# Squares for the guard from GpSimd to ScalarE, with GpSimd's queue and one VectorE step in another order, in an attention kernel between two spectral layers

## The chip, the cores and the metric

The kernel runs on one core of a Trainium2 chip. The metric is device time in microseconds (us) of one execution. Of the core's engines, TensorE (PE in the profile) multiplies into PSUM, ScalarE (ACT) takes exponentials, VectorE (DVE) does most elementwise work, GpSimd (POOL) does elementwise work between SBUF tensors, and SyncE (SP) issues nearly all DMAs.

## The reference

`x` is 8 batches of 512 tokens of 256 numbers. Everything is float32.

```python
x = x + 0.5 * ffn(layernorm(x))      # ffn: FFT over the 256, times a complex 256x256 matrix, real part of the inverse FFT, + bias
x = x + attention(layernorm(x))      # 16 heads of 8, on the left 128 columns; out @ Wo.T (128 -> 256) + bo
x = x + 0.5 * ffn(layernorm(x))
# attention: q, k, v = left @ Wq.T, left @ Wk.T, left @ Wv.T; softmax(q.k / 4) over all 512 keys; times v
```

## The kernel before

The complex matrix is turned once, at the start, into one real 256x256 matrix `half_ffn`, so that each ffn layer is a plain matrix product of 128x256 token tiles (jobs `F1_0` to `F1_3` for the first layer, `F2_0` to `F2_3` for the last, four tiles to a batch).

**Iterations and slots.** The main loop has 8 iterations, one for the attention of each batch. An iteration has 16 slots, one for each group of four heads and 128 keys. In slot `s` TensorE issues the scores of slot `s + 1` (`score_quad`, L768), then the jobs that the table `STEADY` (`BEGIN` in iteration 0, `END` in iteration 7) names for the slot, then the product of the exponentials of slot `s` with the values (`value_quad`, L781). ScalarE takes two exponentials of 128x1024 a slot (L637). There are three score buffers, so the scores of a slot wait for the first exponential of the slot before it.

**What a slot's jobs belong to.** Iteration `it` finishes batch `it - 1` (`WO_0` to `WO_3`, the output projection, in slots 2 and 3, `F2_0` to `F2_3` in slots 9 to 13), projects and checks batch `it + 1` (`QT_0` and `QT_1` in slots 7 and 8 make q, `N` in slot 10 and `NT` in slot 11 make a bound on its scores, and the two guards behind slot 12 branch on it), and begins batch `it + 2` (`F1_0` to `F1_3` in slots 0 to 6, its layernorm, and k in slots 14 and 15 by `KT_0` and `KT_1`). A job's result lies in one PSUM bank, `misc`; the jobs of a slot wait until VectorE has emptied it of those of the slot before (`evacuated`), and `NT` waits for the reduction `norms` (L981) that empties `N`.

**The guard.** `N` multiplies the bf16 squares of q and k (`sq_q`, `sq_k`) by a matrix of ones. Before, GpSimd makes the squares (`square`, L538, 128x512); each waits for VectorE's (`split`, L929) copies of q or k to SBUF.

**GpSimd's other work**, in an order written out by hand in its program, each step waiting for what it reads: `rstd_of(k, n)` (L527 and L529) is the power -0.5 of a variance, for the first (k = 0), the second (1) or the last (2) layernorm; `end_of(b)` (L542 and L532, 128x512 each) makes `x_out` from `x2` and a bias; `begin_x2(b)` (L542 and L532) makes `x2` from `x1` and a bias; `next_x(b)` (L542 and L532) adds a bias to an input.

**The left half.** VectorE normalizes the left 128 columns of batch `it + 2` in `left_half` (L903, four tiles of 128x128 into `lh`, two in slot 8 and two in slot 9, behind its wait for `rstd_of(1, it + 3)`), and turns them in `turn_left` (L912, into `left_blocks`). SyncE's queue, in program order, has `q_out` (q of batch `it + 1` to memory), `left_through` (L445, waits for `turn_left`), four DMAs of q back as rows (`q_rows`, L381, into `QS`), `leftT_in` (L452, which `KT_0` waits for), and four more `q_rows`. The scores of the next iteration's slot 0 wait for all of `QS` and `KS`.

**Divisions.** `normalize(it, 0)` (L1003, L1006: reciprocal, and product of `ot_t` and it into `on`) belongs to the first half of the attention output, which VectorE has turned in slot 7 and which is wanted after slot 15.

Of the kernel before, what the change touches and what calls it, by code (L numbers as in the profile page):

```python
# [25 lines left out]
ACT = mybir.ActivationFunctionType  # L26
AX = mybir.AxisListType

B, S, E = 8, 512, 256
# [3 lines left out]
T = S // P  # L33
# [18 lines left out]
PAIRS = 2 * QUADS  # L52
# [63 lines left out]
def evac_count(name, b):  # L116

    return INDEX[name, b] + 1
# [58 lines left out]
def build_macaron(nc, x, x_t, wq_t, wk_t, wv_t, wo_rows, bo, w_re, w_im, bias, cos_var, sin_tab, ident_in,  # L177
# [14 lines left out]
    with ctx:  # L192
# [44 lines left out]
        qp = sb("qp", [P, PARTS, S])  # L237
        kp = sb("kp", [P, PARTS, S])
        sq_q = sb("sq_q", [P, S], BF16)
# [95 lines left out]
        def wait(eng, s, value):  # L335

            if value > 0:
                eng.wait_ge(s, value)
# [174 lines left out]
        def _(pool):  # L513
# [22 lines left out]
            def square(parts, sq, step, b):  # L536
                pool.wait_ge(step, 2 * (b + 1))
                nc.gpsimd.tensor_tensor(sq[:, :], parts[:, 0, :], parts[:, 0, :], ALU.mult).then_inc(sq_done, 1)  # L538
# [4 lines left out]
                add_row(dst, src, row, done, slice(2, T))  # L543

            def end_of(b):
                wait(pool, out_stored, 32 * b)
                add_rows(x_out, x2, half_bias, x2b_done)

# [26 lines left out]
            pool.wait_ge(late_loaded, 32)  # L575
            begin_x2(0)
            next_x(2)
            square(kp, sq_k, kp_step, 1)
            square(qp, sq_q, qp_step, 1)
            rstd_of(1, 3)  # L580
            next_x(3)
            square(kp, sq_k, kp_step, 2)
            for it in range(1, B):
                rstd_of(2, it)
                if it + 2 < B:
                    rstd_of(1, it + 3)
                end_of(it - 1)
                if it + 1 < B:
                    square(qp, sq_q, qp_step, it + 1)
                begin_x2(it)  # L590
                if it + 3 < B:
                    next_x(it + 3)
                if it + 2 < B:
                    square(kp, sq_k, kp_step, it + 2)
            pool.wait_ge(out_stored, 32 * (B - 1))
            for i in range(2):
                pool.wait_ge(evacuated, evac_count(f"WO_{2 * i + 1}", B - 1))
# [4 lines left out]
        @block.scalar  # L602
        def _(act):
            act.dma_start(cos_var_sb[:, :, :], cos_var.rearrange("(c p) e -> p c e", p=P)).then_inc(re_loaded, 16)
            act.dma_start(sin_sb[:, :, :], sin_tab.rearrange("(c p) e -> p c e", p=P)).then_inc(im_loaded, 16)
            act.dma_start(bias_raw[:, :], bias.partition_broadcast(P)).then_inc(bias_loaded, 16)

            act.wait_ge(waking_set, 1)
            nc.scalar.activation(probs[0][:, 0, 0:32], waking[:, 0:32], ACT.Exp, scale=SCORE_SCALE)

            for piece, bank, copy in ((1, scores[0][:, 0], even[0]), (3, scores[1][:, 0], even[1])):
                act.wait_ge(ffn_mm, piece)
                nc.scalar.copy(copy[:, :, :], half_bank(bank)).then_inc(ffn_copied, 1)
            act.wait_ge(bias_loaded, 16)
            nc.scalar.mul(half_bias[:, :], bias_raw[:, :], 0.5).then_inc(bias_set, 1)
            for piece, bank, copy in ((5, scores[0][:, 0], even[2]), (6, scores[0][:, 1], odd)):
                act.wait_ge(ffn_mm, piece)
                nc.scalar.mul(copy[:, :, :], half_bank(bank), 0.5 / E).then_inc(ffn_copied, 1)


            act.wait_ge(misc_ready, ready_count("QT", 0))
            nc.scalar.copy(qp[:, 0, :].bitcast(F32R), bank_of("QT", 0)).then_inc(qp_step, 2)
            act.wait_ge(evacuated, evac_count("QT", 0))
            store_q(act)
            act.wait_ge(k_stored, 16)
            for lane in range(2, LANES):
                k_rows(act, 0, slice(0, 1), lane, first_rows_in)
            act.wait_ge(q_stored, 16)
            for lane in range(2, LANES):
                q_rows(act, 0, slice(0, 1), lane, first_rows_in)  # L630
            for lane in range(2, LANES):
                k_rows(act, 0, slice(1, SLOTS), lane, second_rows_in)

            for u in range(PAIRS * B):
                act.wait_ge(scores_ready, u // 2 + 1)
                wait(act, quad_done, (u - PRING) // 2 + 1)
                nc.scalar.activation(probs[u % PRING][:, :, :], scores[u % SRING][:, :, :], ACT.Exp,  # L637
                                     scale=SCORE_SCALE).then_inc(exp_done, 1)
            for i in range(2):
                act.wait_ge(lastT_ready, i + 1)  # L640
                nc.scalar.copy(xT[:, :, :, 2 * i:2 * i + 2, :].rearrange("p c g t s -> p (c g) (t s)"),
                               scores[0][:, i, :].rearrange("p (k s) -> p k s", s=2 * 32)).then_inc(lastT_copied, 1)
# [240 lines left out]
        def _(dve):  # L883
# [271 lines left out]
            for it in range(B):  # L1155
                for s in range(QUADS):
                    run_jobs(it, s)
                    if s == 7:
                        take_values(it, 0)
                    if s == 15:  # L1160
                        take_values(it, 1)
                    if s == 14:
                        normalize(it, 0)
                    if s == 0 and it >= 1:
                        normalize(it - 1, 1)
                    if it >= 1:
                        if s == 4:
                            for t in range(2):
                                norm_stats(2, x2, t, False)
                        if s == 5:  # L1170
                            for t in range(2, T):
                                norm_stats(2, x2, t, t == T - 1)
                            norm_moments(2, it)
                    else:
                        if s == 0:
                            norm0_stats(2, range(0, 2))
                        if s == 1:
                            norm0_stats(2, range(2, T))
                            norm_moments(0, 3)
                    if it + 2 < B:  # L1180
                        if s == 8:
                            left_half(it + 2, range(0, 2 if it else T))
                        if s == 9 and it:
                            left_half(it + 2, range(2, T))
                        if s == (9 if it else 8):
                            turn_left(it + 2)
                    if it + 3 < B:
                        if s == 11:
                            norm0_stats(it + 3, range(0, 2))
                        if s == 13:  # L1190
                            norm0_stats(it + 3, range(2, T))
                            norm_moments(0, it + 4)
                    if s == GUARD_SLOT and it + 1 < B:
                        guard(it + 1)
# [59 lines left out]
```

## Time and profile before

| | |
|---|---|
| runs | 338.58, 969.81 and 336.59 us, median 338.58 |
| the profiled execution | 335.66 us, its span 333.9 us |
| engine busy, share of span | PE 91%, ACT 75%, DVE 62%, POOL 34% |
| granted TensorE clock | full speed in all 40 slices |
| DMA | 50.40 MB, 151 GB/s on average; the packets of queue 1 take 52.1% of the 16 DMA engines' span |

The span is the time between the first and last instruction of the profiled execution; 1.8 us of its time lie outside. The main loop's slot-0 scores start at 35.0 us in iteration 0, and its last ones at 317 us, so that 85% of the span is main loop. An iteration of the steady kind (1 to 5) takes 36.4 to 37.5 us.

### The profile page before, as it was taken

The numbers are of one execution on the slowest core, as the hardware profiler recorded it, in microseconds if no ns is written. First come the engines' busy times: TensorE is split into PE (matmuls) and PEld (weight loads), VectorE is DVE, ScalarE is ACT, GpSimd is POOL, SyncE is SP. The second block draws the span as 40 slices with busy tenths as digits, with TensorE's granted clock in tenths as the row PEclk, the third lists the DMA queues.
The fourth block names the chain that finished last, engine by engine and source line by source line (L and its number), as shares of the span: only waits on it lengthen the run. The fifth ranks groups of instructions, "written<-read, shape, count | busy, mean of one in ns | idle before, by whom it ended". The sixth has DMA issues, their size and how long they took to land.

```text
span 333.9 us, 8968 instructions
## 1 busy us (share of the span) xinstructions
PE 302.7 (91%) x3477; PEld 115.7 (35%) x3481; DVE 208.2 (62%) x543; ACT 250.0 (75%) x266; POOL 112.6 (34%) x126
## 2 busy tenths in 40 slices
PE   8887799899988998989989998999988979898985
PEld 5543233234323332333323333343333223232333
DVE  2676656466886679676876778667955723461154
ACT  2100697998977889778978889798977997999921
POOL 5740461310635028140725036230901071007004
PEclk9999999999999999999999999999999999999999
DMA  7636959629535755748645955666354954112001
GB/s 207 221 128 198 183 130 246 194 85 167 204 135 145 186 141 213 213 141 156 232 128 157 167 146 209 203 161 127 128 159 161 139 160 146 65 41 87 33 34 63
DMA packets 30389, 50.40 MB, mean 151 GB/s; under 512 B 3841, under 2 KB 16513, under 8 KB 29441
## 3 DMA queue, kind: packets, MB, share of 16 engines
q1 hardware_dynamic: 28864, 48.13, 52.1%
q10 hardware_dynamic: 1472, 1.58, 2.1%
q8 instruction: 32, 0.52, 0.7%
q14 instruction: 21, 0.16, 0.2%
HBM read 31.87 MB, written 17.83 MB: 149 GB/s over the span
## 4 chain that ended last, share of the span: by engine, by line
PE 51%; DVE 16%; DMA 15%; SPq 7%; issue 6%; ACT 3%; POOL 1%; DVEq 0%; ACTq 0%; POOLq 0%
PE misc L687 20%; PE ot L781 18%; PE scores L768 9%; SPq L381 6%; DVE lh L903 6%; DMA QS<-q_scr 4%; DMA xT<-x_scr 3%; DMA leftT<-left_scr 3%; DMA x_scr<-x_blocks 3%; ACT probs L637 2%; DMA x_in<-x 2%; DVE left_blocks L912 2%; PE scores L687 2%; DVE stats L885 1%; POOL rstd L529 1%
## 5 line engine op out<-in xcount | busy, mean ns | idle before, releaser
L637 ACT ACTIVATE probs<-scores 128x1024 f32<-128x1024 f32 x256 | 244.8, 1027 | 50.4 <-PE scores L768 50.2
L781 PE MATMUL ot<-probs,VS 128*32 128x512 f32 x1024 | 135.6, 595 | 5.0 <-ACT probs L637 3.7
L768 PE MATMUL scores<-QS,KS 32*128 32x512 f32 x512 | 65.0, 495 | 4.6 <-DMA QS<-q_scr 3.7
L527 POOL TENSOR_SCALAR veps<-mv 128x4 f32<-128x4 f32 (+1 forms) x25 | 5.7, 227 | 171.9 <-DVE mv L892 171.9
L768 PEld LDWEIGHTS scores<-QS,KS 32*128 32x128 f32 x512 | 24.7, 181 | 111.8 <-ACT probs L637 96.1
L781 PEld LDWEIGHTS ot<-probs,VS 128*32 128x32 f32 x1024 | 31.1, 109 | 28.4 <-ACT probs L637 9.4
L687 PE MATMUL misc<-half_ffn,xT 128*32 128x256 f32 x448 | 31.4, 385 | 8.0 <-DVE norms L981 6.0
L963 DVE SCALAR_TENSOR_TENSOR x_out<-misc,rstd,x_out 128x256 f32<-128x256 f32 x28 | 13.5, 482 | 33.6 <-PE misc L687 27.4
L687 PE MATMUL misc<-half_ffn,xT_in 128*32 128x256 f32 x400 | 27.9, 385 | 1.4 <-DVE half_ffn L1130 1.3
L903 DVE TENSOR_SCALAR lh<-x,mv,rstd 128x128 f32<-128x128 f32 x32 | 26.2, 868 | 1.8 <-POOL rstd L529 1.8
L529 POOL TENSOR_TENSOR rstd<-veps,power 128x4 f32<-128x4 f32 (+1 forms) x25 | 25.2, 1008 | 2.1
L885 DVE BATCH_NORM_STATS2 stats<-x 128x6 f32<-128x256 f32 x64 | 23.4, 412 | 0.1
L939 DVE SCALAR_TENSOR_TENSOR x<-misc,rstd,x_in 128x256 f32<-128x256 f32 x24 | 11.6, 484 | 15.2 <-PE misc L687 15.2
L958 DVE TENSOR_TENSOR x<-misc,x 128x256 f32<-128x256 f32 x30 | 11.3, 420 | 15.3 <-PE misc L687 15.3
L687 PEld LDWEIGHTS misc<-half_ffn,xT 128*32 128x32 f32 x448 | 11.4, 108 | 19.1 <-DVE norms L981 7.6
L532 POOL TENSOR_TENSOR x_out<-x,half_bias 128x512 f32<-128x512 f32 x9 | 11.5, 1283 | 17.9 <-DVE x L958 17.9
L998 DVE STREAM_TRANSPOSE ot_t<-ot 128x512 f32<-128x512 f32 x16 | 11.4, 714 | 9.0 <-PE ot L781 9.0
L687 PE MATMUL misc<-wo_sb,otn 128*32 128x256 f32 x240 | 16.1, 385 | 0.6 <-DVE otn L1012 0.6
L918 DVE STREAM_TRANSPOSE x_blocks<-x 128x512 f32<-128x512 f32 x14 | 16.2, 1157 | 0.5
L661 PE MATMUL scores<-waking 128*128 128x512 bf16 x49 | 13.0, 412 | 2.5 <-issue 1.3
L538 POOL TENSOR_TENSOR sq_k<-kp 128x512 bf16<-128x512 f32 x8 | 8.3, 1041 | 18.2 <-DVE kp L929 18.2
L687 PEld LDWEIGHTS misc<-half_ffn,xT_in 128*32 128x32 f32 x400 | 10.3, 109 | 11.0 <-issue 5.4
(111 smaller groups left out, 273.3 us busy)
## 6 DMA issues: line engine op xcount, KB each, us to landing
KS<-k_scr SPq DMA_DIRECT2D x56, 128.0 KB, 4.9
QS<-q_scr SPq DMA_DIRECT2D x56, 128.0 KB, 3.3
x_in<-x SPq DMA_DIRECT2D x8, 512.0 KB, 6.0
xT_in<-x_t SPq DMA_DIRECT2D x8, 512.0 KB, 6.8
k_scr<-kp SPq DMA_DIRECT2D x8, 512.0 KB, 2.6
q_scr<-qp SPq DMA_DIRECT2D x7, 512.0 KB, 3.4
x_scr<-x_blocks SPq DMA_DIRECT2D x7, 512.0 KB, 3.6
xT<-x_scr SPq DMA_DIRECT2D x7, 512.0 KB, 4.6
```

What stands on the lines that cost most here:

```text
L381: eng.dma_start(QS[par][first:ROWS * (lane + 1):PARTS, slots, :], q_scr[:, :, heads, :].rearrange("i d h s -> (i d) h s")).then_inc(loaded ...
L529: nc.gpsimd.tensor_tensor(to[:, tiles], veps[k][:, tiles], power[:, tiles], ALU.pow).then_inc(rstd_done[k], 1)
L637: nc.scalar.activation(probs[u % PRING][:, :, :], scores[u % SRING][:, :, :], ACT.Exp, scale=SCORE_SCALE).then_inc(exp_done, 1)
L661: mm(bank, waking[:, 0:P], waking[:, :], start=True, stop=True)
L687: last = mm(dst[COL * j:COL * (j + 1), :], weights(j), rhs, start=c == 0, stop=c == len(terms) - 1)
L768: last = mm(scores[(u + j // 2) % SRING][:, j % 2, :], KS[b % 2][rows, slot, kt * P:(kt + 1) * P].bitcast(F32R), QS[b % 2][rows, slot, :]. ...
L781: last = mm(ot[COL * j:COL * (j + 1), :], VS[b % 2][:, kt, h, :], probs[(u + j // 2) % PRING][:, j % 2, :], start=s % 8 == 0, stop=s % 8 == 7)
L885: ins = nc.vector.bn_stats(stats[k][:, t, :], src[:, t, :])
L903: last = nc.vector.tensor_scalar(lh[:, t, :], x1[b % 3][:, t, 0:HD], mv[1][:, t, 0:1], rstd[1][0][:, t:t + 1], ALU.subtract, ALU.mult)
L918: last = nc.vector.transpose(x2_blocks[:, :, 2 * i:2 * i + 2, :], x2[:, 2 * i:2 * i + 2, :].rearrange("p t (f k) -> p k t f", k=E // 32))
L939: return nc.vector.scalar_tensor_tensor(x1[b % 3][:, i, :], tile, rstd[0][b % 2][:, i:i + 1], biased[:, i, :], ALU.mult, ALU.add)
L963: nc.vector.scalar_tensor_tensor(x_out[:, i, :], tile, rstd[2][0][:, i:i + 1], x_out[:, i, :], ALU.mult, ALU.add).then_inc(evacuated, 1)
```

## The change

Three things are changed. First, the squares of batches 1 to 7 leave GpSimd: ScalarE makes each by one `Square` activation, in iteration `it` for batch `it + 1`, that of k ahead of the exponentials of slot 2 (slot 4 in iteration 0) and that of q ahead of those of slot 10 (slot 6 in iteration 0). Second, in GpSimd's loop `end_of` comes ahead of `rstd_of(2, it)` and waits for `WO_3`, and `begin_x2` comes directly behind that, ahead of `rstd_of(1, it + 3)`. Third, VectorE does `normalize(it, 0)` in slot 12 and no longer in slot 14.

```diff
             def end_of(b):
+                pool.wait_ge(evacuated, evac_count(f"WO_{T - 1}", b))
                 wait(pool, out_stored, 32 * b)
                 add_rows(x_out, x2, half_bias, x2b_done)
...
             next_x(2)
-            square(kp, sq_k, kp_step, 1)
-            square(qp, sq_q, qp_step, 1)
             rstd_of(1, 3)
             next_x(3)
-            square(kp, sq_k, kp_step, 2)
             for it in range(1, B):
+
+                end_of(it - 1)
                 rstd_of(2, it)
+                begin_x2(it)
                 if it + 2 < B:
                     rstd_of(1, it + 3)
-                end_of(it - 1)
-                if it + 1 < B:
-                    square(qp, sq_q, qp_step, it + 1)
-                begin_x2(it)
                 if it + 3 < B:
                     next_x(it + 3)
-                if it + 2 < B:
-                    square(kp, sq_k, kp_step, it + 2)
...
+            def square(parts, sq, step, b):
+                act.wait_ge(step, 2 * (b + 1))
+                nc.scalar.activation(sq[:, :], parts[:, 0, :], ACT.Square).then_inc(sq_done, 1)
+
             for u in range(PAIRS * B):
+                it, s = divmod(u, PAIRS)
+                if it + 1 < B:
+
+                    if s == (2 * 2 if it else 2 * 4):
+                        square(kp, sq_k, kp_step, it + 1)
+                    if s == (2 * 10 if it else 2 * 6):
+                        square(qp, sq_q, qp_step, it + 1)
                 act.wait_ge(scores_ready, u // 2 + 1)
...
-                    if s == 14:
+                    if s == 12:
                         normalize(it, 0)
```

GpSimd's queue in iteration 1, before, from the last square of iteration 0 to the start of `next_x`. `veps` and `rstd` rows are `rstd_of`, `x_out<-x` is `end_of`, `x<-x_1,bo_sb` is `begin_x2`.

```order
L538 TENSOR_TENSOR sq_k<-kp 128x512
L527 TENSOR_SCALAR veps<-mv 128x4
L529 TENSOR_TENSOR rstd_0<-veps,power 128x4
L527 TENSOR_SCALAR veps<-mv 128x4
L529 TENSOR_TENSOR rstd_0<-veps,power 128x4
L542 TENSOR_TENSOR x_out<-x,half_bias 128x512
L532 TENSOR_TENSOR x_out<-x,half_bias 128x512
L538 TENSOR_TENSOR sq_q<-qp 128x512
L542 TENSOR_TENSOR x<-x_1,bo_sb 128x512
L532 TENSOR_TENSOR x<-x_1,bo_sb 128x512
L527 TENSOR_SCALAR veps<-mv 128x4
```

The same place in the changed kernel:

```order
L542 TENSOR_TENSOR x_out<-x,half_bias 128x512
L532 TENSOR_TENSOR x_out<-x,half_bias 128x512
L527 TENSOR_SCALAR veps<-mv 128x4
L529 TENSOR_TENSOR rstd_0<-veps,power 128x4
L542 TENSOR_TENSOR x<-x_1,bo_sb 128x512
L532 TENSOR_TENSOR x<-x_1,bo_sb 128x512
L527 TENSOR_SCALAR veps<-mv 128x4
L529 TENSOR_TENSOR rstd_0<-veps,power 128x4
L527 TENSOR_SCALAR veps<-mv 128x4
```

The power that the left half waits for (the second `rstd` row of each) now stands behind all four large additions of the iteration, where it stood ahead of them, and nothing stands between it and the `veps` of `next_x`.

ScalarE's queue from its last DMA of the start to iteration 2; a row with x16 is eight slots of exponentials. The lines marked - are before, those marked + the changed kernel.

```order
 L374 DMA KS<-k_scr 16x3x512 x4
-L637 ACTIVATE probs<-scores 128x1024 x256
-L641 COPY xT<-scores 128x8x64 x2
+L643 ACTIVATE probs<-scores 128x1024 x8
+L631 ACTIVATE sq_k<-kp 128x512
+L643 ACTIVATE probs<-scores 128x1024 x4
+L631 ACTIVATE sq_q<-qp 128x512
+L643 ACTIVATE probs<-scores 128x1024 x24
+L631 ACTIVATE sq_k<-kp 128x512
+L643 ACTIVATE probs<-scores 128x1024 x16
+L631 ACTIVATE sq_q<-qp 128x512
```

Fourteen squares stand among the exponentials, where there was nothing, and no other row is new.

VectorE's queue at the end of an iteration (slots 13 to 15), before:

```order
L963 SCALAR_TENSOR_TENSOR x_out<-misc,rstd_0,x_out 128x256
L885 BN_STATS stats<-x_in 128x6 x2
L892 BN_AGGR mv<-stats 128x2 x4
L929 CAST kp<-misc 128x256
L931 TENSOR_TENSOR kp<-misc,kp 128x256
L1003 RECIPROCAL recip<-ot_t 128x32
L1006 TENSOR_TENSOR on<-ot_t,recip 128x16x16
L929 CAST kp<-misc 128x256
```

The same place in the changed kernel:

```order
L969 SCALAR_TENSOR_TENSOR x_out<-misc,rstd_0,x_out 128x256
L891 BN_STATS stats<-x_in 128x6 x2
L898 BN_AGGR mv<-stats 128x2 x4
L935 CAST kp<-misc 128x256
L937 TENSOR_TENSOR kp<-misc,kp 128x256
L935 CAST kp<-misc 128x256
```

The two rows of `normalize` have left the place between the two halves of k; they stand one slot after `NT`, ahead of the branch of the guard.

## Rows read from the trace of the kernel before

**Rows 1.** The profile's page: busy time, share of the span, instructions.
```profile
PE 302.7 (91%) x3477; PEld 115.7 (35%) x3481; DVE 208.2 (62%) x543; ACT 250.0 (75%) x266; POOL 112.6 (34%) x126
```

**Rows 2.** Waits of the whole execution: us in total, times, longest.
```profile
PEld scores L768 <- DMA QS<-q_scr: 8.1, 6, 2.5
...
PE misc L687 <- DVE norms L981: 6.0, 5, 1.3
```

**Rows 3.** Timeline of TensorE, iteration 2: start us, us, what, [idle before <-releaser].
```profile
131.68 0.51 PE L768 MATMUL scores<-QS,KS 32*128 32x512 f32 x4
...
135.11 0.51 PE L768 MATMUL scores<-QS,KS 32*128 32x512 f32 x4
...
139.71 0.51 PE L768 MATMUL scores<-QS,KS 32*128 32x512 f32 x4
...
143.26 0.50 PE L768 MATMUL scores<-QS,KS 32*128 32x512 f32 x4 [1.62 <-DMA QS<-q_scr]
```

**Rows 4.** Timeline of VectorE, iteration 2, slots 8 to 10.
```profile
126.68 0.42 DVE L929 CAST qp<-misc 128x256 fp32r<-128x256 f32 x1 [0.29 <-PE misc L687]
...
127.48 2.03 DVE L903 TENSOR_SCALAR lh<-x,mv,rstd 128x128 f32<-128x128 f32 x2
129.43 0.47 DVE L963 SCALAR_TENSOR_TENSOR x_out<-misc,rstd,x_out 128x256 f32<-128x256 f32 x1
129.83 2.17 DVE L903 TENSOR_SCALAR lh<-x,mv,rstd 128x128 f32<-128x128 f32 x2
132.03 1.10 DVE L912 STREAM_TRANSPOSE left_blocks<-lh 128x512 f32<-128x512 f32 x1
133.04 0.39 DVE L981 TENSOR_REDUCE norms<-misc 128x1 f32<-128x256 f32 x1
```

**Rows 5.** Timeline of GpSimd, iteration 2, slots 6 to 10.
```profile
122.94 1.04 POOL L529 TENSOR_TENSOR rstd<-veps,power 128x4 f32<-128x4 f32 x1
...
124.90 1.02 POOL L529 TENSOR_TENSOR rstd<-veps,power 128x4 f32<-128x4 f32 x1
125.90 1.29 POOL L542 TENSOR_TENSOR x_out<-x,half_bias 128x512 f32<-128x512 f32 x1
...
130.60 1.30 POOL L532 TENSOR_TENSOR x<-x,bo_sb 128x512 f32<-128x512 f32 x1
```

**Rows 6.** Line L903 in iteration 0 (GpSimd idle), then 88 to 250 us: duration ns min/median/max.
```profile
L903 DVE TENSOR_SCALAR lh<-x,mv,rstd x4: 341/343/347, 57.1 to 57.8; 128x128 f32<-128x128 f32 x4
...
L903 DVE TENSOR_SCALAR lh<-x,mv,rstd x20: 922/1056/1323, 90.5 to 241.3; 128x128 f32<-128x128 f32 x20
```

**Rows 7.** Timeline of the DMA issues of SyncE, iteration 2.
```profile
133.15 0.33 SPq L445 DMA_DIRECT2D left_scr<-left_blocks  x1
133.53 3.05 SPq L381 DMA_DIRECT2D QS<-q_scr  x4
136.69 0.52 SPq L452 DMA_DIRECT2D leftT<-left_scr  x1
```

**Rows 8.** ScalarE's groups of instructions: count, busy us, mean ns of one.
```profile
L609 ACT ACT_TABLE_LOAD x1 | 1.3, 1283 | 2.3 <-issue 2.3
...
L622 ACT CAST qp<-scores 128x512 fp32r<-128x512 f32 x1 | 0.6, 586 | 12.5 <-PE scores L687 12.5
```

**Rows 9.** Timeline of ScalarE, iteration 2.
```profile
124.23 5.71 ACT L637 ACTIVATE probs<-scores 128x1024 f32<-128x1024 f32 x6 [0.35 <-PE scores L768]
130.29 3.88 ACT L637 ACTIVATE probs<-scores 128x1024 f32<-128x1024 f32 x4 [0.35 <-PE scores L768]
135.67 1.94 ACT L637 ACTIVATE probs<-scores 128x1024 f32<-128x1024 f32 x2 [1.50 <-PE scores L768]
```

**Rows 10.** Timeline of iteration 4, slot 9 and the turn behind it.
```profile
202.55 1.07 PE L687 MATMUL misc<-half_ffn,xT 128*32 128x256 f32 x16 [0.34 <-DMA xT<-x_scr]
...
206.27 1.10 DVE L912 STREAM_TRANSPOSE left_blocks<-lh 128x512 f32<-128x512 f32 x1
```

## The prediction, as it was put on record

> **What bounds the kernel now.** First the busy shares of the page: TensorE has 91% and ScalarE 75% [rows 1], so time is won only where TensorE waits, and work given to ScalarE must fit into what it has left. Then the waits of the whole execution [rows 2], for what TensorE waits for and how often. Two waits recur once an iteration: for the rows of q (`QS`), 8.1 us in six waits of the weight loads that go ahead of the scores, and for `norms`, 6.0 us in five. Then the timelines of one iteration, of which I take iteration 2.
>
> In TensorE's timeline [rows 3] slots 12 and 13 are two undisturbed slots with 16 job multiplications: 139.71 - 135.11 = 4.60, 2.30 us each. Slot 11 is a light one, but takes 135.11 - 131.68 = 3.43 us. Slot 14, with eight job multiplications, takes 143.26 - 139.71 = 3.55 us, and its row says that the scores had waited 1.62 us for `QS`. Without a wait a light slot goes by ScalarE: six exponentials in a row take 5.71 us [rows 9], so two take 1.90.
>
> VectorE's timeline [rows 4] shows what both waits hang on. In slots 8 and 9 it makes the four tiles of the left half, 2.03 and 2.17 us for two each, then turns them until 133.13, and only then takes `norms`, until 133.43, which frees `misc` for the jobs of slot 11. SyncE stores `left_blocks` at 133.15, and the first `QS` rows, which stand behind that store in its queue, go out at 133.53, `leftT` at 136.69, the last `QS` rows behind it [rows 7]. The last of them lands just ahead of 143.26. So from the end of the turn to the next iteration it is 143.26 - 133.13 = 10.1 us, in which nothing is waited for but transfers, and an iteration of the steady kind is as long as this chain makes it.
>
> And the left half is slow for one reason. A tile took 0.343 us in iteration 0, where GpSimd did nothing, and 1.056 us in the median of the twenty of iterations 1 to 5 [rows 6]. GpSimd is without a pause in its additions and a square from 125.90 to 130.60 + 1.30 = 131.90 [rows 5], and the tiles run from 127.48 to 132.00. So a tile waits for GpSimd's instructions, some three times its own time. Other VectorE work that lies beside GpSimd's, as the evacuation of 0.47 us at 129.43, isn't longer.
>
> **GpSimd's new order.** In iteration 2 `rstd_of(2)` ends at 122.94 + 1.04 = 123.98 [rows 5]. Now `end_of` is done before it, in slots 3 and 4, and `begin_x2` follows: two additions of 1.25 us from start to start, until 126.5. Then `rstd_of(1)`, 0.3 us for `veps` and 1.02 for the power: 127.8. That is 1.9 us later than its 125.92. VectorE is free for the left half at 127.5, so the first pair begins 0.3 us later, at 127.85. From there GpSimd has nothing to do until `next_x` in slot 13, since the squares are gone. The pair takes 0.6 us (0.343, and the next some 0.25 behind it, as the four of iteration 0 start from 57.1 to 57.8), until 128.45. The second pair stands behind the evacuation of `F2_0`, which the first pair no longer holds up; TensorE's product for it ends about 129.0, so it is emptied by 129.5. Second pair until 130.05, turn of 1.10 us [rows 4] until 131.2. Before it was 133.13: **1.9 us earlier**.
>
> `norms` is then done at about 131.6, while the jobs of slot 11 want it at 131.68 + 0.45 [rows 3]: that wait is gone, and slot 11 falls from 3.43 to about 2.1 us, a gain of 1.3. The q rows come 1.9 us earlier, so the next iteration can begin at 141.35. TensorE by itself would be there at 139.71 - 1.3 + 1.9 = 140.3. What is late next is therefore the same chain, and the iteration is shorter by the whole 1.9 us, 1.3 in slot 11 and 0.6 in slot 14. The first q rows can't be read before q itself is in memory; they were issued 6 us behind the last copy of q, and I take that a store of a few us is done 4 us behind it as well.
>
> This holds for iterations 1, 2, 3 and 5, 4 x 1.9 = 7.6 us. In iteration 4 `F2_0` waited for `xT` and began at 202.55 [rows 10]. It is emptied by 204.15 whatever GpSimd does, so the turn ends at 205.85 and not at 206.27 + 1.10 = 207.37: 1.5 us. Iteration 0 has fast tiles already [rows 6], and iterations 6 and 7 have no left half: nothing. **Sum 9.1 us.** The Trainium skill (GPSIMD Engine Reference, Key points) has the contention with VectorE only for instructions in a two-port mode or with two SBUF inputs. By that rule the turns of `x2` in slots 2 and 3, which now meet `end_of`, are slowed only if they run in such a mode, which no row here shows; see the third rival.
>
> **The squares on ScalarE.** The trace has no square on this engine. The nearest row is its copy of 128x512 in 0.586 us [rows 8]; exponentials of 1.03 us in the mean stand 0.95 apart in a row (5.71 / 6), so I take 0.51 us for one among others. The lower bound is the same copy without its start, some 0.43, the upper one 0.59: 14 squares are 6 to 8.3 us of ScalarE. What lies over them: a full slot takes 2.30 us and its two exponentials 1.90 to 1.94, so that ScalarE idles some 0.35 us ahead of a pair [rows 9], and the next scores need the first exponential alone. The square of k stands ahead of slot 2, at the beginning of five to seven such slots; it pushes the exponentials by 0.15 to 0.2 us, which nobody waits for and the next gap takes back. **Nothing.** The square of q stands in the run of six exponentials from 124.23, ahead of its fifth, at 128.04. It waits for the copy of q, which ends at 126.68 + 0.42 = 127.10 [rows 4], so there is 0.9 us to spare. It pushes the run by 0.51, of which 0.35 is the gap before the next run [rows 9], and the remaining 0.2 lies in slots 10 to 13, where the chain of the q rows sets the end. **Nothing**; without that cover it would be 0.2 an iteration. `N` needs the square in slot 10, two slots of exponentials before which it is done. In iteration 6 slots 0 and 1 are ScalarE's, and I put 0.2 us there. Off GpSimd the squares give nothing of their own beyond what the left half was given above. The Trainium skill (ScalarE: Activation LUTs, Rules for kernel authors) speaks against this: `mul` belongs on VectorE, not ScalarE. By its formula in "What ACT_TABLE_LOAD costs" a square of 512 is about 0.61 us, an estimate, near the row's 0.586; 14 of them with no cover would take all but some 0.6 us of the gain.
>
> **The division in slot 12.** Two VectorE rows leave slot 14 for slot 12, where VectorE has nothing but an evacuation of 0.47 us in 2.30. In slot 14 they lay between the two halves of k, but the second half is multiplied only behind the scores at 143.26 [rows 3], when they were done. Nothing. The new wait on `WO_3` holds only GpSimd's own queue, which had to wait for the same data anyway.
>
> So 9.1 - 0.2 = 8.9 us, against the profiled execution's 335.66: 326.8. The other two undisturbed runs are 336.59 and 338.58; I take 336.6 as what the kernel before does, which gives **327.6 us**, 2.7% less. A measurement of this kernel can tell about 2% from no change.
>
> **The rivals.**
> First, the transfers don't follow. Between the turn and the last q row lie a store, a load and eight row loads with the DMA engines half busy; moved up by 1.9 us they meet more of the loads of `x` and the store of q. If each iteration loses 0.9 of its 1.9 us, 5 x 0.9 = 4.5, it is 332. For it: this chain measured from 9 to 10 us in different iterations. Against: its steps are mostly the fixed time of an issue and a landing. If nothing of slot 14 moves at all and the chain ends where it did, it eats the gain of slot 11 too, and the time is 336.6.
> Second, ScalarE becomes the bound, on the other side. Place: the run from slot 8 to slot 12. Price: 14 x 0.59 = 8.3 us with none covered; it decides from the point where the square of q is reached before its copy is there, that is if VectorE is over 0.9 us later than now, or the chain of the q rows is not what ends the iteration. Without any gain elsewhere that is 344.9. For it: 75% busy, and six exponentials in a row with no gap. Against: gaps of 0.35 and 1.50 us on both sides [rows 9]. A harder form is that a square throws out the table of the exponential. A table load took 1.283 us [rows 8]; two to a square and the square itself are 14 x 3.15 = 44 us, less 9 of gain: 372. Against: the changed program has no more such loads in ScalarE's queue than the one before. The same page of the Trainium skill (Table sets: the hidden batching unit) has a load at a switch to another set only, puts relu, copy, identity and abs into every set, and doesn't say of square; by its figure of about 2.66 us for each switch it would be more than this.
> Third, `end_of` beside the turns of `x2`. No such turn lay beside GpSimd's work in this trace. If VectorE's turn waits as a tile does, `x2` is out up to 1.1 us later, and so is `xT` at `F2_0`: 1.1 in iterations 4 and 6, which wait for it already, and little in the others: 2.5 us, 330.1.
> Fourth, the q rows come even sooner, because the later part of the chain took 10.1 us in iteration 2 and may take 9 everywhere: some 3 us more, 324.5.
>
> **How the numbers follow.** Forecast 0.66 (its own range 325 to 330), transfers that follow in part 0.12 (332), not at all 0.07 (336.6), the turns 0.05 (330.1), ScalarE as the bound 0.04 (344.9), table loads 0.02 (372), better 0.04 (324.5). The range 324 to 333 takes in the forecast, the fourth, the third and the partial one, 0.87. Faster by over 2% is below 329.9: nearly all of the forecast, the fourth, and parts of the first and third, 0.74; slower 0.06; the rest 0.20.
>
> **What would show it.** Tiles of the left half at 0.34 us, no wait for `norms`, slot 11 near 2.1 us, the first q rows 1.9 us earlier against slot 8, squares of 0.5 to 0.6 us on ScalarE with no table load, `begin_x2` between the two powers. What would make it wrong: a wait for `QS` that grows by as much as the one for `norms` shrinks, slots 8 to 11 longer than 1.9 us with ScalarE full, or longer turns of `x2`.

## The result and the profile after

The changed kernel takes 327.62 us in the median of four runs (326.72 to 328.11). The kernel before took 336.59, 338.58, 353.86 and 969.81 us, and ratios, here and below, leave out runs over 1.5% above the fastest of their kernel, here the last two, while times are medians of all runs. The ratio is 0.9702 with a 95% interval of 0.9641 to 0.9762: 3.0% faster. A second set of six runs of the same kernel, further down, gives 0.9743 (0.9684 to 0.9803). The forecast was 327.6 us and 2.7%. The profiled execution took 327.63 us, 8.0 less than the 335.66 of the one before.

The page of the changed kernel, part 1, answers to [rows 1]:

```profile
PE 302.9 (93%) x3477; PEld 116.5 (36%) x3481; DVE 191.9 (59%) x543; ACT 255.4 (78%) x280; POOL 97.7 (30%) x112
```

GpSimd has 14 instructions less and is busy 14.9 us less, ScalarE 14 more and 5.4 us longer. VectorE has the instructions that it had, and yet is busy 16.3 us less: most of it are the twenty tiles of the left half, which [rows 6] has at 1.06 us.

The waits, to [rows 2] (us in total, times, longest):

```profile
PEld scores L774 <- DMA QS<-q_scr: 5.9, 6, 1.7
...
PE misc L693 <- DMA leftT<-left_scr: 2.7, 4, 1.1
...
PE scores L774 <- DMA QS<-q_scr: 1.7, 2, 0.9
...
PE misc L693 <- DMA xT<-x_scr: 1.7, 2, 1.0
```

The row of `norms` is gone, that of `QS` is smaller and still the largest of this kind, and `leftT` has 2.7 us. That last wait isn't new. The kernel before had it too, with one wait less, in a row that [rows 2] leave out:

```profile
PE misc L687 <- DMA leftT<-left_scr: 2.5, 3, 1.5
```

VectorE's tiles, to [rows 6], for 88 to 250 us:

```profile
L909 DVE TENSOR_SCALAR lh<-x,mv,rstd x20: 339/343/350, 91.2 to 234.5; 128x128 f32<-128x128 f32 x20
```

All twenty take the 0.34 us that those of iteration 0 took. Iteration 2 on VectorE, to [rows 4]; its slot-0 scores are at 104.61 (105.73 before):

```profile
126.70 0.61 DVE L909 TENSOR_SCALAR lh<-x,mv,rstd 128x128 f32<-128x128 f32 x2 [0.27 <-POOL rstd L529]
127.88 0.48 DVE L969 SCALAR_TENSOR_TENSOR x_out<-misc,rstd,x_out 128x256 f32<-128x256 f32 x1 [0.58 <-PE misc L693]
128.28 0.59 DVE L909 TENSOR_SCALAR lh<-x,mv,rstd 128x128 f32<-128x128 f32 x2
128.91 1.17 DVE L918 STREAM_TRANSPOSE left_blocks<-lh 128x512 f32<-128x512 f32 x1
129.99 0.41 DVE L987 TENSOR_REDUCE norms<-misc 128x1 f32<-128x256 f32 x1
```

The turn ends 130.08 - 104.61 = 25.47 us into the iteration; before it was 133.13 - 105.73 = 27.40. So it is 1.93 us earlier, and 1.9 was forecast. TensorE, to [rows 3]:

```profile
130.55 0.51 PE L774 MATMUL scores<-QS,KS 32*128 32x512 f32 x4
132.61 0.51 PE L774 MATMUL scores<-QS,KS 32*128 32x512 f32 x4
134.90 0.50 PE L774 MATMUL scores<-QS,KS 32*128 32x512 f32 x4
137.19 0.51 PE L774 MATMUL scores<-QS,KS 32*128 32x512 f32 x4
138.23 0.64 PE L693 MATMUL misc<-leftT,wk_sb 128*32 128x256 f32 x8 [0.53 <-DMA leftT<-left_scr]
139.66 0.51 PE L774 MATMUL scores<-QS,KS 32*128 32x512 f32 x4
```

Slot 11 takes 132.61 - 130.55 = 2.06 us, where it took 3.43. Slot 14 takes 139.66 - 137.19 = 2.47, where it took 3.55, and what its row names now is `leftT`, not `QS`. The last q row isn't far off: issued at 135.8, it lands 9.3 us behind the turn, at 139.4. So without the wait for `leftT` the slot-0 scores could have begun some 0.25 us earlier, not more. GpSimd and ScalarE in the same stretch:

```profile
125.30 0.24 POOL L527 TENSOR_SCALAR veps<-mv 128x4 f32<-128x4 f32 x1
125.63 1.04 POOL L529 TENSOR_TENSOR rstd<-veps,power 128x4 f32<-128x4 f32 x1
```

```profile
123.09 3.80 ACT L643 ACTIVATE probs<-scores 128x1024 f32<-128x1024 f32 x4 [0.35 <-PE scores L774]
126.78 0.63 ACT L631 ACTIVATE sq_q<-qp 128x512 bf16<-128x512 f32 x1
127.30 7.82 ACT L643 ACTIVATE probs<-scores 128x1024 f32<-128x1024 f32 x8
135.47 1.94 ACT L643 ACTIVATE probs<-scores 128x1024 f32<-128x1024 f32 x2 [0.35 <-PE scores L774]
```

GpSimd's last work ahead of the tiles ends at 126.67. The square of q stands among the exponentials without a gap on either side, 0.63 us long by its record, and moves them by 127.30 - 126.78 = 0.52 us, where 0.51 was taken. There is no table load beside it. It turns the runs of six and four exponentials into one of twelve with the square in it, from 123.09 to 135.12, and only behind that is ScalarE waiting again. The turns of `x2`, half of which now lie beside `end_of`, took 1.15 to 1.18 us, and 1.14 to 1.17 before.

The slot-0 scores of iterations 1 to 6 stand at 69.10, 104.61, 139.66, 174.87, 209.91 and 246.24; before, at 68.79, 105.73, 143.26, 179.99, 216.41 and 253.83. Iterations 1 to 5 took 177.1 us together and took 185.0 before: 7.9 us of the 8.0.

### The profile page after: what moved, and what is told of

Same layout as the page of the kernel before. It is cut to its first block, busy times and chain, and to the rows that moved or that the text cites. A ratio compares the mean times of both kernels' runs of the same rounds, so it can differ in the third digit from the quotient of the medians.

```text
span 325.8 us, 8974 instructions
## 1 busy us (share of the span) xinstructions
PE 302.9 (93%) x3477; PEld 116.5 (36%) x3481; DVE 191.9 (59%) x543; ACT 255.4 (78%) x280; POOL 97.7 (30%) x112
## 4 chain that ended last, share of the span: by engine, by line
PE 61%; DMA 12%; DVE 10%; issue 6%; SPq 5%; ACT 4%; POOL 1%; DVEq 0%; ACTq 0%; POOLq 0%
PE misc L693 22%; PE ot L787 21%; PE scores L774 11%; DMA leftT<-left_scr 6%; SPq L381 4%; ACT probs L643 4%; DMA xT<-x_scr 3%; DVE lh L909 2%; PE scores L660 2%; DVE left_blocks L918 2%; PE scores L693 2%; DMA x_scr<-x_blocks 1%; PE scores L667 1%; DMA QS<-q_scr 1%; DVE stats L891 1%
## 5 line engine op out<-in xcount | busy, mean ns | idle before, releaser
L542 POOL TENSOR_TENSOR x_out<-x,half_bias 128x512 f32<-128x512 f32 x7 | 9.0, 1291 | 98.5 <-DVE x L964 98.5
L969 DVE SCALAR_TENSOR_TENSOR x_out<-misc,rstd,x_out 128x256 f32<-128x256 f32 x28 | 13.5, 484 | 34.6 <-PE misc L693 25.6
L945 DVE SCALAR_TENSOR_TENSOR x<-misc,rstd,x_in 128x256 f32<-128x256 f32 x24 | 11.6, 484 | 15.1 <-PE misc L693 15.1
L532 POOL TENSOR_TENSOR x_out<-x,half_bias 128x512 f32<-128x512 f32 x9 | 11.5, 1282 | 20.6 <-DVE x L964 20.6
L1004 DVE STREAM_TRANSPOSE ot_t<-ot 128x512 f32<-128x512 f32 x16 | 11.4, 715 | 10.2 <-PE ot L787 10.2
L924 DVE STREAM_TRANSPOSE x_blocks<-x 128x512 f32<-128x512 f32 x14 | 16.3, 1162 | 0.5
L693 PEld LDWEIGHTS misc<-half_ffn,xT 128*32 128x32 f32 x448 | 11.4, 108 | 12.4 <-issue 8.4
L935 DVE CAST kp<-misc 128x256 fp32r<-128x256 f32 x14 | 5.9, 424 | 16.6 <-PE misc L693 16.6
```

The lines of the kernel that those rows point to most:

```text
L532: nc.gpsimd.tensor_tensor(dst[:, tiles, :], src[:, tiles, :], row[:, :].unsqueeze(1).to_broadcast([P, tiles.stop - tiles.start, E]), ALU.a ...
L693: last = mm(dst[COL * j:COL * (j + 1), :], weights(j), rhs, start=c == 0, stop=c == len(terms) - 1)
L924: last = nc.vector.transpose(x2_blocks[:, :, 2 * i:2 * i + 2, :], x2[:, 2 * i:2 * i + 2, :].rearrange("p t (f k) -> p k t f", k=E // 32))
L945: return nc.vector.scalar_tensor_tensor(x1[b % 3][:, i, :], tile, rstd[0][b % 2][:, i:i + 1], biased[:, i, :], ALU.mult, ALU.add)
L969: nc.vector.scalar_tensor_tensor(x_out[:, i, :], tile, rstd[2][0][:, i:i + 1], x_out[:, i, :], ALU.mult, ALU.add).then_inc(evacuated, 1)
```

## The experiments

Theory A is the prediction's: the tiles of the left half are slow beside GpSimd's work, and the chain of transfers behind them sets the length of an iteration. Its rivals are that the squares themselves were what counted (B), that GpSimd's earlier results were (C), and that ScalarE's time counts wherever a square stands (D). The kernels of one group ran on the same chip beside the kernel before: the first four below, then the changed kernel once more with the one without squares and the first two on transfers, then the last two on transfers with the division in its old place. Every ratio is to that, with its 95% interval.

### GpSimd's order without the squares' move

```diff
 # the changed kernel, but in the program of GpSimd
                 begin_x2(it)
                 if it + 2 < B:
                     rstd_of(1, it + 3)
+                if it + 1 < B:
+                    square(qp, sq_q, qp_step, it + 1)
                 if it + 3 < B:
                     next_x(it + 3)
+                if it + 2 < B:
+                    square(kp, sq_k, kp_step, it + 2)
 # ... and no squares in that of ScalarE
```

> The changed kernel with the squares back on GpSimd: that of q behind rstd_of(1), that of k at the end of the iteration; GpSimd's new order and the division in slot 12 stay. Theory A (the tiles of the left half are slow beside GpSimd's work, and the chain behind them sets the length of an iteration): one square of 1.04 us lies beside the first pair of tiles alone, whose time is hidden until F2_0 is evacuated, so nearly all of the gain stays, 327.6 to 328.8 us. Theory B (the gain is that GpSimd and N get rid of the squares): 334 to 337 us.

329.04 us, ratio 0.9771 (0.9722 to 0.9820). Nearly all of the gain is there. Of an iteration's four tiles the first alone is slow, as the maximum shows, and the time of the first pair is hidden until `F2_0` comes:

```profile
L905 DVE TENSOR_SCALAR lh<-x,mv,rstd x20: 330/334/1060, 90.6 to 234.0; 128x128 f32<-128x128 f32 x20
```

Theory B falls as the explanation of the whole gain. What the move of the squares gives beside the order is less than these runs can tell.

### The squares' move without GpSimd's order

```diff
 # the changed kernel, but in the program of GpSimd
             for it in range(1, B):
-                end_of(it - 1)
                 rstd_of(2, it)
-                begin_x2(it)
                 if it + 2 < B:
                     rstd_of(1, it + 3)
+                end_of(it - 1)
+                begin_x2(it)
 # ... and normalize(it, 0) back in slot 14
```

> The squares on ScalarE, but GpSimd's order and the place of the division as before the change. Theory A: end_of and begin_x2 still lie beside the left half, 5.1 us of them and no longer 6.0, so the turn ends some 0.9 us earlier than before in each of five iterations: 336.6 - 4.5, 331 to 333 us. Theory B: all of the gain, about 327.6 us.

333.56 us, ratio 0.9879 (0.9832 to 0.9926), between both kernels, as theory A has it. GpSimd is done one square earlier beside the left half, so that most tiles are slow still, but the last of an iteration are not:

```profile
L908 DVE TENSOR_SCALAR lh<-x,mv,rstd x20: 334/808/1323, 92.3 to 240.6; 128x128 f32<-128x128 f32 x20
```

### Nothing but work for GpSimd beside the left half

```diff
                 if it + 2 < B:
                     rstd_of(1, it + 3)
+                    for n in range(4):
+                        pool.wait_ge(idle_set, 4 * (it - 1) + n + 1)
+                        nc.gpsimd.tensor_tensor(idle[:, :], idle_in[:, :], idle_in[:, :], ALU.add).then_inc(idle_set, 1)
```

> The changed kernel with four additions of 128x512 on GpSimd behind rstd_of(1), into a tile that nobody reads, in iterations 1 to 5: nothing waits for them. Theory A: 4 x 1.3 us of GpSimd's work lie beside the left half again, tiles go from 0.34 to some 1.05 us, norms and the q rows are late again: 335 to 337.5 us. Theory C (the gain is that x_out and x2 are ready earlier, or that the powers are): unchanged, 327 to 328 us, since next_x isn't delayed.

337.94 us, ratio 1.0016 (0.9987 to 1.0045). Four additions whose result nobody reads, in a queue that has nothing else to do then, take back the whole gain. The additions stand first, then VectorE's turn in iteration 2, which began at 107.97, and the tiles of iterations 1 to 5, then the waits:

```profile
130.01 4.40 POOL L594 TENSOR_TENSOR idle<-idle_in 128x512 f32<-128x512 f32 x4
```

```profile
134.53 1.09 DVE L925 STREAM_TRANSPOSE left_blocks<-lh 128x512 f32<-128x512 f32 x1
```

```profile
L916 DVE TENSOR_SCALAR lh<-x,mv,rstd x20: 802/1128/1198, 92.3 to 244.9; 128x128 f32<-128x128 f32 x20
```

```profile
PEld scores L781 <- DMA QS<-q_scr: 8.9, 6, 2.4
...
PE misc L700 <- DVE norms L994: 5.8, 5, 1.2
```

The turn ends 135.62 - 107.97 = 27.65 us into the iteration, the 27.40 of the kernel before and a little more, and both waits of [rows 2] are back, though `x_out`, `x2` and all powers are as early as in the changed kernel: in iteration 2 `end_of` starts 11.17 us in (11.16 there), `begin_x2` 18.23 (18.21), and the power for the left half 21.03 (21.02). Theory C falls. This run shows the cause and not only that it fits: the tiles, and with them the time, follow GpSimd's work alone.

### Every square twice

```diff
                 act.wait_ge(step, 2 * (b + 1))
+                nc.scalar.activation(sq_spare[:, :], parts[:, 0, :], ACT.Square)
                 nc.scalar.activation(sq[:, :], parts[:, 0, :], ACT.Square).then_inc(sq_done, 1)
```

> The changed kernel with every square on ScalarE made twice, the first one into a tile that nobody reads. Theory A (a square is covered by ScalarE's gap of 0.35 us a full slot and by the chain of the q rows): 0 to 1.5 us more, 327.5 to 329 us. Theory D (ScalarE is the bound wherever a square stands): 14 x 0.52 = 7.3 us more, 335 us.

329.54 us, ratio 0.9779 (0.9734 to 0.9825). Its profiled execution has the second square in iteration 2, and the slots that it touches:

```profile
127.30 0.63 ACT L632 ACTIVATE sq_spare<-qp 128x512 bf16<-128x512 f32 x1
127.82 0.63 ACT L633 ACTIVATE sq_q<-qp 128x512 bf16<-128x512 f32 x1
128.34 7.59 ACT L645 ACTIVATE probs<-scores 128x1024 f32<-128x1024 f32 x8
136.29 1.94 ACT L645 ACTIVATE probs<-scores 128x1024 f32<-128x1024 f32 x2 [0.36 <-PE scores L776]
```

```profile
126.83 0.50 PE L776 MATMUL scores<-QS,KS 32*128 32x512 f32 x4
...
129.42 0.51 PE L776 MATMUL scores<-QS,KS 32*128 32x512 f32 x4 [0.23 <-ACT probs L645]
...
138.03 0.51 PE L776 MATMUL scores<-QS,KS 32*128 32x512 f32 x4
...
139.90 0.51 PE L776 MATMUL scores<-QS,KS 32*128 32x512 f32 x4
```

Slot 9 takes 129.42 - 126.83 = 2.59 us, not 2.29: 0.3 us in which TensorE waits for an exponential, and so in each of iterations 1 to 5. With 0.35 us in slot 3 of iteration 0 and 0.5 in slot 1 of iteration 6 the fourteen further squares cost TensorE 2.4 us of their 7.3. Slot 14 of iteration 2 then takes 139.90 - 138.03 = 1.87, not 2.47. That it takes the 0.3 us back is likely but not shown by this slot: a second trace of the changed kernel, without a doubled square, has 1.92 there. Over iterations 1 to 5 slot 14 takes 12.3 us here, 13.5 and 12.7 in the two traces of the changed kernel. Theory D (335 us) falls, and the second square is covered for the most part.

### No squares at all

```diff
-                    pe.wait_ge(sq_done, 2 * (b + 1))
+                    pe.wait_ge(sq_done, 2)
 # ... and no squares of batches 1 to 7 in any program
```

> The changed kernel without the squares of batches 1 to 7 on any engine: N multiplies those of batch 0 again, so this part of the computation is left out. Theory A (squares are covered): at most 0.5 us less than the changed kernel, from iteration 6. Theory D (ScalarE's time counts): 14 x 0.52 = 7.3 us less, 320 us.

329.31 us, ratio 0.9763 (0.9700 to 0.9825). The changed kernel itself, once more beside it:

> The changed kernel as it is, beside the next ones on the same chip: 327 to 329 us.

328.83 us, ratio 0.9743 (0.9684 to 0.9803). Without the squares nothing is won that these runs can tell. The one place where a trace has it is slot 1 of iteration 6: 1.87 us without, 2.03 with the square. Slots 9 to 13 of iteration 2, around the square of q, take 10.9 us with it and without it.

### The division back in slot 14

```diff
-                    if s == 12:
+                    if s == 14:
                         normalize(it, 0)
```

> The changed kernel with the division of the first half back in slot 14. Theory A has it at nothing: 327 to 329 us, as the changed kernel. The rival is that it held up the second half of k beside next_x's additions, 0.1 to 1 us an iteration in four to five iterations: 330 to 332 us.

328.34 us, ratio 0.9776 (0.9726 to 0.9826): no difference of its own in the median. But the trace has what the prediction put at nothing. VectorE and GpSimd, and the scores that TensorE issues in slots 0 and 1 of iteration 5, whose slot-0 scores were at 210.79:

```profile
211.23 1.40 DVE L1012 TENSOR_TENSOR on<-ot_t,recip 128x256 f32<-128x256 f32 x1
212.31 1.46 POOL L532 TENSOR_TENSOR x_in<-x_in,half_bias 128x512 f32<-128x512 f32 x1
212.55 0.41 DVE L935 CAST kp<-misc 128x256 fp32r<-128x256 f32 x1
212.65 0.51 PE L774 MATMUL scores<-QS,KS 32*128 32x512 f32 x4
213.00 0.42 DVE L937 TENSOR_TENSOR kp<-misc,kp 128x256 fp32r<-128x256 f32 x1
...
213.48 0.64 PE L693 MATMUL misc<-wv_sb,leftT 128*32 128x128 f32 x16 [0.32 <-DVE kp L937]
...
215.34 0.50 PE L774 MATMUL scores<-QS,KS 32*128 32x512 f32 x4
```

The product `on` takes 1.40 us beside `next_x` (0.42 to 0.43 in all sixteen of the changed kernel), the second half of k waits for it, and slot 0 takes 215.34 - 212.65 = 2.69 us and not 2.30, 0.39 us more. At the start of iterations 3 and 4 it is 0.07 and 0.26 us, of iteration 2 none. It goes with where the product ends: 0.78 us behind the slot-0 scores of iteration 2, then 1.52, 1.71 and 1.84.

### The chain of transfers behind the turn

In the changed kernel slot 14 waits for `leftT` in iterations 2 to 5, the four waits of its row above. Two kernels take up how the transfers stand in their queues.

```diff
                 if it + 1 < B:
-                    q_in(it + 1, range(0, 2))
+                    q_in(it + 1, range(0, 1))
                 if it + 2 < B:
                     leftT_in(it + 2)
                 if it + 1 < B:
-                    q_in(it + 1, range(2, LANES))
+                    q_in(it + 1, range(1, LANES))
```

> The changed kernel with leftT's DMA two q rows earlier in SyncE's queue. In the trace of the changed kernel slot 14 of iterations 2 and 4 ends by leftT, not by the last q row. Theory E (leftT is what ends it there): 0.3 to 0.5 us less in each of two iterations, about 0.8 us in all, no more, since the last q rows come when they came or 0.3 us later. Theory F (the q rows are the bound everywhere): no change or up to 1.5 us more.

326.42 us, ratio 0.9667 (0.9611 to 0.9724), 2.4 us less than the changed kernel of the same group, with intervals that overlap. A second time it was 325.78, 0.9683 (0.9638 to 0.9729):

> The changed kernel with leftT two q rows earlier, once more, as the base of the next one: 325 to 327 us.

Theory F falls. The gain is more than the 0.8 us of theory E, which counted iterations 2 and 4 alone. In the traces slot 14 takes 11.4 and 11.6 us over iterations 1 to 5, where the two of the changed kernel have 13.5 and 12.7: 1.1 to 2.0 us less. The DMA issues, size and median time to landing, of the changed kernel and of this one:

```profile
leftT<-left_scr SPq DMA_DIRECT2D x6, 256.0 KB, 5.1
```

```profile
leftT<-left_scr SPq DMA_DIRECT2D x6, 256.0 KB, 3.3
```

`leftT` isn't only issued earlier, it also lands faster, and no wait for it is left. What ends slot 14 now is the last q row, in each of the five iterations. The second kernel gives four of the eight q rows to GpSimd's queue as well:

```diff
                     rstd_of(1, it + 3)
+                if it + 1 < B:
+                    pool.wait_ge(quad_done, QUADS * it)
+                    pool.wait_ge(q_stored, 16 * (it + 2))
+                    for lane in range(2, LANES):
+                        q_rows(pool, (it + 1) % 2, slice(0, SLOTS), lane, pool_rows_in)
```

> The changed kernel with the last four q rows of an iteration issued by GpSimd, which has nothing to do between the power for the left half and next_x, and with leftT two rows earlier in SyncE's queue. Theory G (the chain is SyncE's issue time, eight rows at 0.6 us): all rows are in before slot 15, slot 14 goes by ScalarE with 1.9 us, and 2.91 + 2.46 + 2.60 + 2.44 + 3.04 - 5 x 1.9 = 4.0 us are won against the changed kernel, 323 to 324 us. Theory H (transfers are limited by the DMA engines or GpSimd's own issue takes as long): 326 to 329 us, or more where GpSimd's issue falls beside the tiles of the left half.

329.72 us, ratio 0.9785 (0.9726 to 0.9845). All is issued by 134.4 in iteration 2, which began at 105.03, and yet slot 14 takes 2.78 us there and waits for `leftT` in every iteration:

```profile
130.42 2.03 POOL L382 DMA_DIRECT2D QS<-q_scr  x4 [3.33 <-DMA q_scr<-qp]
```

```profile
PE misc L703 <- DMA leftT<-left_scr: 3.8, 5, 1.0
```

```profile
QS<-q_scr POOLq DMA_DIRECT2D x28, 128.0 KB, 3.8
QS<-q_scr SPq DMA_DIRECT2D x28, 128.0 KB, 4.5
...
leftT<-left_scr SPq DMA_DIRECT2D x6, 256.0 KB, 5.7
```

A q row of SyncE lands in 4.5 us and not 3.2, `leftT` in 5.7 and not 3.3. The q rows as a whole are in somewhat sooner: the last one lands 8.9 us behind the turn in iteration 2, where it was 9.3 in the changed kernel and 9.1 with `leftT` earlier. But `leftT` lands 8.3 us behind it, where it was 8.0 and 5.4. Theory G, that the issue time is the limit, falls: what is saved in issuing goes into longer transfers (H).

Last, the base with `leftT` earlier, and all four tiles in slot 8:

```diff
-                            left_half(it + 2, range(0, 2 if it else T))
-                        if s == 9 and it:
-                            left_half(it + 2, range(2, T))
+                            left_half(it + 2)
```

> The former with all four tiles of the left half in slot 8, where GpSimd is now idle. Four tiles take 1.2 us, from 0.1 us after the last half of q to just before F2_0 is to be evacuated, so the turn ends about 0.55 us earlier than with two of them behind F2_0. Theory A (the chain from the turn to the last q row sets the iteration): up to 0.5 us less in each of five iterations as far as slot 14 is over ScalarE's 1.9 us, 1.3 us in all, 324.5 to 326 us. Theory I (q's own store, which is done at about the same time, starts the chain): no change.

325.10 us, ratio 0.9646 (0.9596 to 0.9696), the fastest of all. It is 0.7 us below its base, within the intervals, so the times don't decide between theories A and I. The traces say more. The turn ends 24.8 us into each of iterations 1 to 5, 0.7 earlier than in the base (25.5). SyncE's queue in iteration 3, here (slot-0 scores at 140.79, end of the turn at 165.59) and in the base (138.99 and 164.48):

```profile
166.65 1.14 SPq L381 DMA_DIRECT2D QS<-q_scr  x2
```

```profile
164.88 1.14 SPq L381 DMA_DIRECT2D QS<-q_scr  x2
```

The first q row goes out 25.86 us into the iteration and 25.89 in the base: it has gained nothing, since q's own store is done only 1.0 us behind the turn. In iterations 2 and 4 more than half of the 0.7 us is lost in this way, in 1 and 5 none. Iterations 1 to 5 take 173.8 us together and 174.6 in the base: 0.8 less, where theory A had up to 1.3. So each theory holds for a part, and q's store is the next thing in the way.

This is 3.5% less than the kernel before. Against the changed kernel (0.9702, 0.9641 to 0.9762) it is 0.6%, which these runs don't make certain.

## What the prediction had right and what it had wrong, step by step

The mechanism was right. What failed is a size: the term of 9.1 us, and in it the step "the iteration is shorter by the whole 1.9 us, 1.3 in slot 11 and 0.6 in slot 14".

**The bound and the cause** are shown. Tiles at 0.34 us, no wait for `norms`, the turn 1.93 us earlier (1.9), slot 11 at 2.06 us (2.1): each as put down, and the run with idle additions shows that GpSimd's work beside the tiles is the cause.

**What an iteration gains** was mis-sized. Iteration 2 lost 37.53 - 35.05 = 2.48 us, the other four 1.43, 1.52, 1.38 and 1.09, together 7.9 where the term was 9.1. Slot 11 gave its part, 6.4 us in the five. Slot 14 did not: it lost 1.08 us in iteration 2, but 0.06, 0.18, 0.03 and 0.44 in 1, 3, 4 and 5, where 0.6 was put down. The step took the chain from the turn to the next slot-0 scores to stay as long as it was. The sums over iterations 1 to 5, in us, of the kernel before and of two traces of the changed kernel (the second is that of the run beside the one without squares):

| | before | changed | changed, again |
|---|---|---|---|
| slot-0 scores to the end of the turn | 136.9 | 128.1 | 127.3 |
| end of the turn to the next slot-0 scores | 48.1 | 49.0 | 48.4 |
| together | 185.0 | 177.1 | 175.7 |

The turns came 8.8 us earlier, and the chain behind them took 0.9 us more. In the second trace it is 9.6 and 0.3, and the gain is 9.3. So the term was 1.2 us too large for one execution and 0.2 too small for another of the same kernel: the chain in iteration 2 took 10.1 us before, then 9.6 and 9.1. The first rival had this scatter as its reason. Why it varies stays open. Its steps aren't of a fixed time, as the prediction had it: in iterations 1 to 5 of the traces with all q rows on SyncE `leftT` alone took 2.8 to 5.9 us to land.

**What is late next** was given as the q rows alone. In iterations 2 to 5 it was `leftT`, by 0.2 to 0.4 us. It took 5.1 us to land there in the median, and 3.16 in iteration 2 of the kernel before, the one that I had looked at; in iterations 3 to 5 of that kernel it took 4.5 to 5.4 and was waited for already.

**Iteration 4 and `xT`.** The 0.4 us that `xT` cost in iteration 4 of [rows 10] wasn't there; in iteration 5 it was 0.7 us in its place, and in the second trace none. The term of 1.5 us belonged to one execution, not to one iteration.

**The squares** cost nothing where nothing was forecast, and 2.03 - 1.87 = 0.16 us in slot 1 of iteration 6 where 0.2 was. The reason given for the square of q was not the one: its 0.2 us were to be hidden by the chain of the q rows in slot 14, but they never reach TensorE, since slots 9 to 13 take as long without the squares. ScalarE catches up in its own gaps. Only a second square gets through, 0.3 us in slot 9.

**The division** was put at nothing, because the second half of k is multiplied only behind the scores at 143.26, "when they were done". They weren't. The kernel before has, beside `next_x`,

```profile
142.03 1.47 DVE L1006 TENSOR_TENSOR on<-ot_t,recip 128x256 f32<-128x256 f32 x1
```

which ends at 143.50 and takes over three times its own 0.42 us. At the start of iterations 2, 4 and 5 it ends 0.8 to 1.3 us behind the slot-0 scores. It cost nothing there, since VectorE takes the second half of k only at 144.41, and has waited 0.91 us for it by then. In the kernel with the division back in slot 14 and the rest of the change, the product ends up to 1.84 us behind the slot-0 scores, and costs up to 0.4 us in an iteration.

**The sum.** 8.9 us was forecast and 8.0 came in the profiled execution, 335.66 to 327.63. That the time was met to 0.1 us is luck in part: it rests on the start taken as 336.6 (and 336.6 - 8.9 is 327.7). From the profiled execution alone the forecast would have been 326.8; and against the 337.6 that 336.59 and 338.58 have in the mean, 10.1 us were won.

**The rivals.** Neither slower one came: no table load, and ScalarE, with twelve exponentials and a square in a row, still waited behind them. The turns of `x2` didn't get longer beside GpSimd's additions. "Transfers that follow in part" is true by a size: 0.9 us of 9 in one trace, 0.3 in the other.

## What to carry to other kernels

When an instruction takes three times its own time in one place and not in another, look at what a neighbour engine does in those microseconds: work that nobody waits for can cost as much as work on the critical path. Moving it costs nothing if a stretch is free, and the check is an experiment that adds idle work there. One trace is one execution: a term that is read from a single iteration of it should be read from all of them, and from a second trace where there is one. And an edit costed at nothing because a wait covers it has to be costed again against the profile in which the other edits have removed that wait.

## What the runs showed of the hardware

- Beside GpSimd's additions between SBUF tiles, a VectorE `TENSOR_SCALAR` of 128x128 float32 in SBUF took 1.06 us in the median for 0.34 (kernel before), and a `TENSOR_TENSOR` of 128x256 in SBUF 1.16 to 1.46 for 0.42 (division back in slot 14). Not longer were evacuations from PSUM with one SBUF operand (0.48 us), `BATCH_NORM_STATS2` (0.41) and 32x32 transposes of 128x512 between SBUF tiles (1.17 for 1.16), of which the kernel before had shown nothing. The Trainium skill (GPSIMD Engine Reference, Key points) has contention for two-port modes and two SBUF inputs. The `TENSOR_TENSOR` with two SBUF inputs agrees with it; for the `TENSOR_SCALAR`, with one, it would take a two-port mode, which no row here shows.
- A `Square` of 128x512 to bf16 on ScalarE had a record of 0.63 to 0.64 us and cost 0.52 between exponentials, without a table load.
- How long a DMA takes to land depends on what is issued around it: `leftT` (256 KB) took 3.3 us in the median with two q rows ahead of it in its queue, 5.1 with four, and 5.7 with two ahead and four more from a second queue at the same time. The q rows on SyncE went from 3.2 to 4.5 us in that last case.
